# Merged DMA transposes, a wider fp16 ring and a moved copy of x in a cross-attention and routed-FFN kernel

## What is computed

```python
# x: (1, 1024, 128), context q: (1, 6404, 128)
c = layernorm(x)
s = (c @ w_c + b_c)[:, :, None] + (q @ w_q + b_q)[:, None, :] + einsum('bcd,bqd,d->bcq', c, q, w_cq) + b_cq
a = softmax(s, axis=2)
c2q_att = a @ q
b_att = softmax(max(s, axis=2), axis=1)
q2c_att = einsum('bc,bcd->bd', b_att, c)
x = x + concat([c, c2q_att, c * c2q_att, c * q2c_att]) @ W_l.T + b_l
n = layernorm(x)
expert_id = argmax(n @ wr + br)             # 8 experts
x = x + (gelu(n @ w1[e] + b1[e]) @ w2[e] + b2[e]) for e = expert_id of each row
```

## Time and profile before

| | before |
|---|---|
| median of 3 runs | 235.63 us (235.04 to 236.16) |
| the profiled execution's own time | 233.51 us |
| its span | 231.8 us |
| TensorE busy | 198.0 us (85%) |
| VectorE busy | 180.0 us (78%) |
| ScalarE busy | 158.0 us (68%) |
| GpSimd busy | 130.5 us (56%) |
| hardware DMA queue of SyncE | 49.56 MB, 93.2% of the 16 engines' span |

### The profile page before, as it was taken

One profiled execution on the slowest core, in us unless ns is written; L12 is line 12 of the kernel. 1 busy time (PEld: TensorE's weight loads), 2 busy tenths in 40 slices (PEclk: granted clock), 3 DMA queues, 4 the chain that ended last, 5 costly groups with the idle time before them and its releaser, 6 DMA issues.

```text
span 231.8 us, 5012 instructions
## 1 busy us (share of the span) xinstructions
PE 198.0 (85%) x1837; PEld 148.7 (64%) x1837; DVE 180.0 (78%) x393; ACT 158.0 (68%) x249; POOL 130.5 (56%) x179
## 2 busy tenths in 40 slices
PE   0298798995999969999999999899993799799970
PEld 0133356663676736776866767789983799789960
DVE  2789997995997994997997998958847447567770
ACT  2750799994799689399699699689432355667630
POOL 4699405999607987505906988654400740037783
PEclk9999999999999988999999999999995579999997
DMA  6999999899999999999989999969992459999200
GB/s 206 382 277 247 192 298 244 182 221 201 262 193 254 226 203 226 267 170 243 245 193 261 209 204 225 212 141 210 237 285 78 146 200 296 370 365 382 71 21 0
DMA packets 141918, 51.25 MB, mean 221 GB/s; under 512 B 121156, under 2 KB 139733, under 8 KB 141894
## 3 DMA queue, kind: packets, MB, share of 16 engines
q1 hardware_dynamic: 140960, 49.56, 93.2%
q0 software_dynamic: 784, 1.38, 1.7%
q10 hardware_dynamic: 150, 0.00, 0.0%
HBM read 10.22 MB, written 3.75 MB: 60 GB/s over the span
## 4 chain that ended last, share of the span: by engine, by line
PE 42%; DVE 22%; DMA 12%; issue 11%; ACT 9%; POOL 3%; DVEq 0%; ACTq 0%; POOLq 0%
DMA PT<-Phl 10%; DVE S L792 5%; PE psX L1075 5%; PE psS L1055 5%; PE psS L1057 5%; PE psS L1056 5%; ACT S L646 5%; DVE Phl L809 4%; PE psO L1075 4%; ACT Phl L661 3%; PE psS L1288 3%; PE psX L1077 3%; POOL out_x L603 2%; PE psS L1274 2%; PE psO L1077 2%
## 5 line engine op out<-in xcount | busy, mean ns | idle before, releaser
L646 ACT ACTIVATE S<-S,negb 128x1024 f32<-128x1024 f32 x48 | 55.0, 1145 | 14.6 <-DVE negb L800 14.6
L792 DVE TENSOR_SCALAR_CACHE_REDUCE S<-psS 128x1024 f32<-128x1024 f32 x48 | 58.2, 1216 | 8.2 <-PE psS L1057 7.7
L809 DVE TENSOR_TENSOR Phl<-S,Phl 128x1024 f16<-128x1024 f32 x38 | 50.9, 1340 | 7.7 <-ACT Phl L661 7.6
L661 ACT CAST Phl<-S 128x1024 f16<-128x1024 f32 x48 | 50.2, 1045 | 6.1 <-DMA PT<-Phl 4.7
L533 POOL TENSOR_TENSOR Phl<-S,Phl 128x256 f16<-128x256 f32 x40 | 26.2, 685 | 48.6 <-ACT Phl L661 48.6
L1055 PE MATMUL psS<-qT,gh 128*128 128x512 f16 x96 | 37.8, 394 | 3.3 <-DVE gl L769 2.7
L1075 PE MATMUL psO<-qn,PT 128*128 128x256 f16 x204 | 37.4, 277 | 2.5 <-DMA PT<-Phl 2.4
L1075 PE MATMUL psX<-qn,PT 128*128 128x256 f16 x204 | 36.4, 273 | 2.6 <-DMA PT<-Phl 2.6
L1056 PE MATMUL psS<-qT,gh 128*128 128x512 f16 x96 | 37.7, 392 | 0.0
L1057 PE MATMUL psS<-qT,gl 128*128 128x512 f16 x96 | 37.7, 392 | 0.0
L1077 PE MATMUL psO<-qn,PT 128*128 128x128 f16 x204 | 36.0, 222 | 0.0
(11 more groups left out here) (239 smaller groups left out, 424.9 us busy)
## 6 DMA issues: line engine op xcount, KB each, us to landing
PT<-wp SPq DMA_DIRECT2D x8, 512.0 KB, 4.9
stageT<-in_ctxT SPq DMA_DIRECT2D x6, 512.0 KB, 7.3
qn<-wp SPq DMA_DIRECT2D x6, 512.0 KB, 6.8
wp<-in_w SPq DMA_DIRECT2D x4, 512.0 KB, 4.8
stageT<-in_w SPq DMA_DIRECT2D x4, 512.0 KB, 4.7
rows_by_expert<-stageT SPq DMA_DIRECT2D x4, 385.5 KB, 5.3
PT<-Phl SPq DMA_TRANSPOSE x48, 4.1
S<-rows_by_expert SPq DMA_DIRECT2D x2, 258.0 KB, 5.6
```

The lines of the kernel that those rows point to most:

```text
L646: nc.scalar.activation(slot(t, e), slot(t, e), ACT.Exp, bias=negb[:, t:t + 1], accum_out=Lp[:, t * NG + e:t * NG + e + 1]).then_inc(exp_do ...
L661: nc.scalar.copy(hi, slot(t, e)).then_inc(high_done, 1)
L792: nc.vector.tensor_scalar(out=into, in0=bank(u, n)[:, 0:into.shape[1]], scalar1=1.0 / GS, scalar2=None, op0=ALU.mult, op1=ALU.max, accum_o ...
L809: nc.vector.tensor_tensor(lo, slot(t, e), hi, ALU.subtract).then_inc(low_done, 1)
```

## The change

1. `Phl` holds six pieces and the tail side by side, a place for each piece of a row tile. The 8 KB per partition for it come from the scratch of dynamic DMAs (8192 instead of the default). high(t, e) now waits for the landing of the transpose that took the same piece of row tile t-1.
2. A transpose takes a unit: pieces 0 and 1, pieces 2 and 3, pieces 4 to 6 (in the last row tile 4, and 5 with 6). The issue waits for the low halves of all of the unit's pieces, and each W waits for its whole unit. 25 transposes of P take the place of 56, and 4 of the context that of 7.
3. ScalarE copies x into `x_re`; GpSimd adds b_l in place later, behind low(1, 3). evict(1, 1) waits for the copy, not for the sum.
4. Two loads of w1 are issued before the transposes of the context; the load of w2 that belongs to row tile t (1 to 4) is issued behind the last unit of row tile t.

```diff
-        Phl = sb("Phl", [P, PARTS, 2, GR], F16)
-        Ptail = sb("Ptail", [P, 2, TAILP], F16)
+        PW = 2 * GR
+        Phl = sb("Phl", [P, (NG - 1) * PW + 2 * TAILP], F16)
+        Ptail = Phl[:, (NG - 1) * PW:].rearrange("p (a w) -> p a w", a=2)
...
+        QN_UNITS = ((0, 2), (2, 4), (4, 6), (6, 7))
...
+        def pT_units(t):
+
+            return ((0, 2), (2, 4), (4, 5), (5, NG)) if t == T - 1 else ((0, 2), (2, 4), (4, NG))
...
-            def transpose(t, e):
-
-                wait_low(sp, t, e)
+            def transpose(t, g):
+
+                e0, e1 = pT_units(t)[g]
+                for e in range(e0, e1):
+                    wait_low(sp, t, e)
                 if t > 0:
-                    sp.wait_ge(pv_done, (t - 1) * NG + e + 1)
-                src, _, _, dst = piece(t, e)
-                sp.dma_start_transpose(dst, src).then_inc(pT_landed[e], 16)
+                    sp.wait_ge(pv_done, (t - 1) * NG + e1)
+                end = (NG - 1) * PW + 2 * TAILP if e1 == NG else e1 * PW
+                n = len([j for e in range(e0, e1) for j in tiles(e)])
+                sp.dma_start_transpose(PT[:, 2 * e0 * TW:2 * (e0 * TW + n), :],
+                                       Phl[:, e0 * PW:end]).then_inc(pT_landed[g], 16)
...
-            for k in range(H - 1):
-                load_w1(k)
+            load_w1(0)
+            load_w1(1)
+            for g, (n0, n1) in enumerate(QN_UNITS):
...
-            for e in range(NG):
-                transpose(0, e)
-            load_w1(H - 1)
-
-            W2_BEHIND = {(1, 5): 0, (2, 3): 1, (3, 1): 2, (4, 1): 3}
-            for t in range(1, T):
-                for e in range(NG):
-                    transpose(t, e)
-                    if (t, e) in W2_BEHIND:
-                        load_w2(W2_BEHIND[t, e])
+            for t in range(T):
+                for g in range(len(pT_units(t))):
+                    transpose(t, g)
+                if t == 0:
+                    load_w1(H - 1)
+                elif t <= H:
+                    load_w2(t - 1)
...
+            pool.wait_ge(qTl_ready, len(DVE_LOW))
             pool.wait_ge(qTl_pool_ready, len(POOL_LOW))
-            pool.wait_ge(qTl_ready, DVE_LOW.index(4) + 1)
-            pool.wait_ge(x_landed, 16)
-            pool.wait_ge(late_landed, 16 * NLATE)
-            nc.gpsimd.tensor_tensor(x_re, x_sb, blr[:, :].unsqueeze(1).broadcast_to([P, T, D]),
-                                    ALU.add).then_inc(x_re_ready, 1)
-            pool.wait_ge(qTl_ready, len(DVE_LOW))
...
             low_piece(1, 3)
+            pool.wait_ge(x_kept, 1)
+            pool.wait_ge(late_landed, 16 * NLATE)
+            nc.gpsimd.tensor_tensor(x_re, x_re, blr[:, :].unsqueeze(1).broadcast_to([P, T, D]),
+                                    ALU.add).then_inc(x_re_ready, 1)
             split(0)
...
             deviation(2, H, T)
+            act.wait_ge(qTl_ready, DVE_LOW.index(4) + 1)
+            act.wait_ge(qTl_pool_ready, POOL_LOW.index(5) + 1)
+            nc.scalar.copy(x_re, x_sb).then_inc(x_kept, 1)
             act.wait_ge(shift_ready, 1)
...
-                past = t * (NG - 1) + e - PARTS
-                if e == NG - 1 and t > 0:
-                    act.wait_ge(pT_landed[e], 16 * t)
+                if t > 0:
+                    act.wait_ge(pT_landed[pT_unit(t - 1, e)], 16 * t)
                 elif e == NG - 1:
                     act.wait_ge(consts_ready, 5)
-                elif past >= 0:
-                    act.wait_ge(pT_landed[past % (NG - 1)], 16 * (past // (NG - 1) + 1))
...
             def weighted(t, e):
 
-                pe.wait_ge(pT_landed[e], 16 * (t + 1))
+                pe.wait_ge(pT_landed[pT_unit(t, e)], 16 * (t + 1 if t < T - 1 or e < 5 else 1))
...
-    nc = _bacc.Bacc("TRN2", target_bir_lowering=False, num_devices=1)
+    nc = _bacc.Bacc("TRN2", target_bir_lowering=False, num_devices=1, dynamic_dma_scratch_size=8192)
```

More of the change, by code:

```diff
@@ L67, in build @@
     SLOTS = 8
-    PARTS = 4
     BANKS = 3
@@ L183, in build @@
         x2T = S[:, 0, :]
-        hf = parts_ring[:, RING * 2 * F:RING * 4 * F].bitcast(F32).rearrange("p (r f) -> p r f", f=F)
+        hf = Phl[:, RING * 2 * F:RING * 4 * F].bitcast(F32).rearrange("p (r f) -> p r f", f=F)
         xTp = S[:, 1:3, :].rearrange("p r w -> p (r w)")[:, 0:(NB + 1) * P].bitcast(F16)\
@@ L201, in build @@
         x_landed = sem("x_landed")
+        x_kept = sem("x_kept")
         x_re_ready = sem("x_re_ready")
@@ L204, in build @@
         qT_landed = [sem(f"qT_landed{n}") for n in range(NG)]
-        qn_landed = [sem(f"qn_landed{n}") for n in range(NG)]
+        qn_landed = [sem(f"qn_landed{g}") for g in range(4)]
         late_landed = sem("late_landed")
@@ L228, in build @@
         exp_done = sem("exp_done")
-        pT_landed = [sem(f"pT_landed{e}") for e in range(NG)]
+        pT_landed = [sem(f"pT_landed{g}") for g in range(4)]
         high_done = sem("high_done")
@@ L320, in columns, with qn_unit, pT_unit @@
             return buf[:, 0, 0:w], buf[:, 1, 0:w]
+        QN_UNITS = ((0, 2), (2, 4), (4, 6), (6, 7))
+        def qn_unit(n):
+            return min(n // 2, 3)
         def rows_of(n):
-            k = len(tiles(n))
-            buf = qT[:, n, :, :] if n < NG - 1 else qTend[:, :, :]
-            return buf.rearrange("p a w -> p (a w)"), qn[:, 2 * n * TW:2 * n * TW + 2 * k, :]
+            return qn[:, 2 * n * TW:2 * n * TW + 2 * len(tiles(n)), :]
+        def pT_units(t):
+            return ((0, 2), (2, 4), (4, 5), (5, NG)) if t == T - 1 else ((0, 2), (2, 4), (4, NG))
+        def pT_unit(t, e):
+            return [e0 <= e < e1 for e0, e1 in pT_units(t)].index(True)
         def pool_low(t, e):
@@ L349, in bank, with piece @@
             return psS[(u * NG + n) % BANKS]
[L351 to L356, removed]
+        def piece(e):
+            w = cols(e, GR)[1] - e * GR
+            buf = Phl[:, e * PW:(e + 1) * PW].rearrange("p (a w) -> p a w", a=2) if e < NG - 1 else Ptail
+            return buf[:, 0, 0:w], buf[:, 1, 0:w]
         def block_w(b):
@@ L402, in load_w2 @@
                              w2[k * n:(k + 1) * n].rearrange("e (k p) d -> p e k d", p=P)).then_inc(w_landed[H + k], 16)
-            for k in range(H - 1):
-                load_w1(k)
+            load_w1(0)
+            load_w1(1)
+            for g, (n0, n1) in enumerate(QN_UNITS):
+                for n in range(n0, n1):
+                    sp.wait_ge(qTh_ready, n + 1)
+                    if n in DVE_LOW:
+                        sp.wait_ge(qTl_ready, DVE_LOW.index(n) + 1)
+                    else:
+                        sp.wait_ge(qTl_pool_ready, POOL_LOW.index(n) + 1)
+                src = qT[:, n0:n1, :, :].rearrange("p n a w -> p (n a w)") if n1 < NG else \
+                    qTend[:, :, :].rearrange("p a w -> p (a w)")
+                k = sum(len(tiles(n)) for n in range(n0, n1))
+                sp.dma_start_transpose(qn[:, 2 * n0 * TW:2 * (n0 * TW + k), :], src).then_inc(qn_landed[g], 16)
+            load_w1(2)
             for r in (0, 32):
@@ L529, in low_piece @@
                 pool.wait_ge(high_done, t * NG + e + 1)
-                _, hi, lo, _ = piece(t, e)
+                hi, lo = piece(e)
                 for a in range(0, GR, CHUNK):
@@ L651, in high @@
                 act.wait_ge(exp_done, t * NG + e + 1)
-                past = t * (NG - 1) + e - PARTS
-                if e == NG - 1 and t > 0:
-                    act.wait_ge(pT_landed[e], 16 * t)
+                if t > 0:
+                    act.wait_ge(pT_landed[pT_unit(t - 1, e)], 16 * t)
                 elif e == NG - 1:
                     act.wait_ge(consts_ready, 5)
-                elif past >= 0:
-                    act.wait_ge(pT_landed[past % (NG - 1)], 16 * (past // (NG - 1) + 1))
-                _, hi, _, _ = piece(t, e)
+                hi, _ = piece(e)
                 nc.scalar.copy(hi, slot(t, e)).then_inc(high_done, 1)
@@ L783, in scores @@
                     dve.wait_ge(c_late_ready, T - H)
-                    dve.wait_ge(x_re_ready, 1)
+                    dve.wait_ge(x_kept, 1)
                 if n == NG - 1 and u >= 2:
@@ L1061, in weighted @@
             def weighted(t, e):
-                pe.wait_ge(pT_landed[e], 16 * (t + 1))
+                pe.wait_ge(pT_landed[pT_unit(t, e)], 16 * (t + 1 if t < T - 1 or e < 5 else 1))
                 if t == 0:
-                    pe.wait_ge(qn_landed[e], 16)
+                    pe.wait_ge(qn_landed[qn_unit(e)], 16)
                 if t == 0 and e == 0:
@@ L1072, in weighted @@
                 n, acc = len(tiles(e)), psA[t % 2]
-                both = rows_of(e)[1].rearrange("p (a j) d -> p a j d", a=2)
+                both = rows_of(e).rearrange("p (a j) d -> p a j d", a=2)
                 for i, j in enumerate(tiles(e)):
```

11 lines of the change are left out of this document (1 added, 10 removed).

## The result

The changed kernel takes 249.39 us (median of 4 runs, 247.27 to 249.69), the kernel before 235.66 in the same session: a ratio of 1.0565, 95% interval 1.050 to 1.063. It is slower, as forecast, but by 13.7 us instead of 4.0, and above the range. The profiled execution took 249.69 us with a span of 248.0. The ratios leave out the executions of a kernel that are over 1.5% longer than its fastest; the profiled executions of experiments 1 and 8 are of these.

What follows compares the result with a forecast made beforehand. TensorE was taken to set the pace in mid-attention. Terms -1.55 + 0.15 + 1.0 - 1.6 + 3.8 + 2.2 = +4.0 on 233.5 gave 237.5, median 239.6 us; range 237 to 242, eight times in ten 230.5 to 244.5.

Steps and rivals of the forecast that it cites:

- What bounds the kernel: Attention: TensorE sets the pace, turns take about 16.6 us; turns 2 and 4 lose 2.5 us each to late transposes.
- the price of 3.7 us for a load: Turns 2 and 4: a 512 KB weight load ahead of a transpose costs that transpose 3.7 us.
- Price of a merged transpose: Transposes of P: fixed 2.0 us plus about 0.1 a block, so 32 blocks land in 5.5 us, 38 in 6.0.
- Rival A: Faster: 38 blocks land within 4.8 us, so W(t,4) never waits; 230.6 us, chance 0.24.
- Rival B: No change: 38 blocks land in 5.1 us, between 4.8 and 5.4, shrinking the wait at W(t,4); 235.4 us, chance 0.14.
- the term for turns 3 to 7: W(t,4) waits 1.25 us for its unit each turn: turn 3 +1.0, turn 4 -1.6, turns 5 to 7 +3.8.
- part 2: Turns 1 and 2: 0; T(2) at 60.6 against 62.0, so the start's 1.4 us is kept.
- part 4: Last row tile: W(6,4) waits for the last unit of row tile 6, 6.95 us after T(7); +2.2 us.
- the gain of the copy of x: Start: without GpSimd's sum there the shift comes 1.55 us earlier, T(0) goes from 28.2 to 26.7.
- Rival C: Slower still: waits let the clock fall, about 1.7 us each, or w2 loads delay first units; 244 us, chance 0.14.
- The ring and the scratch at 0: Turn 2's old loss only changes its cause; smaller scratch at 21 indirect DMAs costs 0, at most some 2 us.
- the early w1 loads: Start: queued ahead of the context's transposes, which W(0,0) needs only 15 us later; cost 0, other bound 3.7 us.

Runs made afterwards that it cites:

- experiment 1: Changed kernel with one transpose for each piece again, of P and of the context: ratio 0.985 to the kernel before.
- experiment 8: Experiment 1 with the first two w1 loads behind the context's transposes: ratio 0.989 to the kernel before.
- experiment 12: Experiment 1 with only pieces 5 and 6 merged in one transpose of 22 blocks: ratio 0.986 to the kernel before, 232.53 us.
- experiment 11: Kernel before with the ring of six and ScalarE's copy of x, single transposes and all loads as before: ratio 0.996.
- experiment 4: Kernel before with only the ring of six places and the tail, and the smaller scratch: ratio 1.000.
- experiment 2: Changed kernel with units (0,1) (2,3) (4,5) (6) in every row tile: ratio 1.028 to the kernel before, 243.15 us.
- experiment 3: Kernel before with only ScalarE's copy of x and GpSimd's sum moved behind low(1, 3): ratio 0.994.
- experiment 6: Changed kernel with the first two w1 loads back behind the context's transposes: ratio 1.059 to the kernel before.
- experiment 10: Experiment 1 with pieces 0 and 1, and pieces 2 and 3, merged: ratio 1.019 to the kernel before, 240.18 us.
- experiment 7: Changed kernel with 64 one-column matmuls on idle TensorE at the start, to move the instruction packets: ratio 1.047 to the kernel before.

## Why the prediction was right in sign and wrong in size

**What bounds the kernel** held: turns of 16.6 us where nothing waits (experiments 1 and 12), and turn 4 lost its time to a transpose with a weight load ahead of it (experiments 1 and 11). In turn 2 the ring passed such a late landing on to ScalarE (experiment 4), though TensorE waited for it as well, 2.37 us at 56.34. But the price of 3.7 us for a load is a wrong reading of the earlier trace rows: both of these transposes also met a packet of the instruction queue, at 53.29 and 82.77. In the DMA view of before from 53.0 to 55.5 us, inside the transpose issued at 49.00, the same stop stands as in the changed kernel:

```profile
DMA  9999999990100100100901001000001049999999
GB/s 414 266 274 274 524 250 262 258 61 8 12 8 8 12 8 8 12 8 12 16 8 12 8 8 12 8 8 8 12 8 12 8 106 279 299 279 307 283 287 287
...
q8 instruction: 1, 0.02, 2.4%
```

Two transposes of before with a load ahead and no packet, issued at 90.74 and 107.51, landed in 5.4 and 6.0 us. The second:

```profile
PT<-Phl SPq DMA_TRANSPOSE x1, 6.0
```

So a load ahead costs about 2 us, and the rest of the 3.7 is the packet.

**Price of a merged transpose:** 5.5 and 6.0 forecast for 32 and 38 blocks, 5.6 to 5.8 and 6.2 to 6.4 measured where nothing disturbs them. The upper figure for contiguous transposes in the Trainium skill (DMA: Bandwidth & Descriptors, Latency and other measured facts), weighed in the prediction, is not borne out: the stream stays at 280 to 290 GB/s in the long ones. Rivals A and B, which needed a landing under 4.8 or 5.4, fall with this.

**The step that failed** is the term for turns 3 to 7 (and with it parts 2 and 4): it took the landing of a lone transpose for that of all. The trace of before already held the other kind. Over the transposes of P in the profile of before, the 16 with an instruction packet in flight landed in 5.3 us by median, the 40 without in 3.9; in the changed kernel 7 take 7.7 and 18 take 5.9. Of the 16 in before ten still landed 1.0 to 3.3 us ahead of the first matmul of their W. The last unit of the change has nothing to spare: TensorE waits for it even when it is on time (1.08 and 1.13 us), and a packet in it adds 1.4 us (7.7 against 6.3) or 2.5 us (8.8). The lost 12 us of span beyond the forecast 4, from the table and the rows above:

- T(0), +1.0: the gain of the copy of x is there, the twin of L747 takes 0.16 us (timeline below), but T(0) is later than forecast. Experiments 1, 2 and 3 have it at 26.4, 26.7 and 26.8, and over all profiles of kernels with this copy it lies between 26.3 and 27.7, so this is the spread of the start as far as is known. The c_sb on VectorE, 2.24 us at 7.12 instead of 1.47, is not the reason: in experiment 3 it took 2.6.
- Turn 2, +2.3: W(0,0) came at 41.55, forecast 38.8, after 4.96 us of idling. Of these 2.7 us 1.0 is T(0), 1.3 is SyncE, which came to unit (0,0) only after the context's transposes and the third w1 load, and 0.4 the landing. The clock fell to half with it (the first row of the windows below).
- Turns 3 and 4, +2.9: together they took 38.0 us, 4.8 more than two turns of 16.6, and TensorE idled 4.6 us in them: 1.83 ahead of W(1,4), which the prediction had on time, 1.20 ahead of W(2,0) and 1.58 ahead of W(2,4). The unit of W(2,0) stood behind the w2 load and took 9.2 us, with a packet in it at 75.54; the prediction named this bound, up to 1.5 us, and took 0. That of W(2,4) had the packet at 88.86.
- Turn 5, +3.6: the packet in the unit of W(3,4), a wait of 3.73 us, and the clock (second row).
- T(7) to the last W, +1.7: W(6,4) came 6.9 us after T(7), exactly as forecast, but W(7,2) waited 1.30 us for a unit that took 8.2 us with a packet in it. Another 0.7 us went behind the last W, and the reason for it is open.

VectorE's and ScalarE's timeline of the changed kernel at the start (the third and fourth row are the new copy and the c_sb activations behind it):

```profile
7.12 2.24 DVE L771 TENSOR_SCALAR c_sb<-S,mv,rstd 128x128 f32<-128x128 f32 x4
...
22.36 0.16 DVE L761 TENSOR_TENSOR sc<-rstd 128x4 f32<-128x4 f32 x1
...
21.13 1.04 ACT L651 COPY stageT<-S 128x1024 f32<-128x1024 f32 x1 [4.61 <-DVE qT L790]
...
23.35 1.65 ACT L654 ACTIVATE c_sb<-S,sc,rstd 128x128 f32<-128x128 f32 x4 [1.18 <-DVE sc L848]
```

The copy is hidden: 1.18 us of idling are still left behind it. Windows of the changed kernel, columns as in the earlier trace rows:

```profile
38.90:45.80 6.90, 4.25 (x27) 3.45 (x28) 5.78 (x10) 6.50 (x12) 6.40 (x10) 0.51 1.00 227
110.60:114.00 3.40, 2.67 (x17) 2.19 (x18) 0.00 (x0) 3.37 (x5) 2.92 (x6) 0.50 1.05 253
```

The granted clock is at half (1.2 GHz) there; each time it fell in the course of a TensorE wait, those of 4.96 and 3.73 us that ended at 41.55 and 111.33. With the waits of 1.1 to 1.8 us in the other turns it stayed at full (2.4 GHz). Rival C had this mechanism and named two or three falls; it was the nearest case, with two falls in the attention, but its 244 us have no packets in them, and it had a chance of 0.14. Its reading of before is off: the wait that ended at 85.05 and was followed by a fall was 2.23 us long, and the one of 2.4 (2.37 us, at 56.34) was followed by none.

**VectorE's share.** The wait list of the changed kernel shows the same chain from its other end: VectorE now waits for scores, where before had 7.7 us in 7 waits.

```profile
DVE S L806 <- PE psS L1071: 24.4, 19, 5.1
...
PEld psO L1089 <- DMA PT<-Phl: 14.3, 6, 5.0
...
PEld psX L1089 <- DMA PT<-Phl: 10.3, 6, 4.2
```

**The ring and the scratch at 0** held in the whole time (experiment 4). So did the early w1 loads (experiments 6 and 8), but not for the reason given: W(0,0) does not miss the context's transposes, it misses its own, which stand behind them in SyncE's stream (1.3 us late in the change, 4.7 us in experiment 1). The first units' 0.5 us in a turn held (experiment 10); that merging them makes turn 2 3 to 4 us longer did not.

Left open: why turn 3 of experiment 4 takes 17.2 us, why T(0) spreads by more than 1 us, and how much of the packet's cost depends on the place in the transpose at which it falls. A kernel without instruction packets was not tried.

## What to carry to other kernels

Before transfers are merged, take for each the time from the last input to the first use, not the mean load of the queue: a merged transfer is issued with its latest input and needed by its earliest reader, and where that reader sits in the stream of the bounding engine every microsecond is paid each turn. If anything, merge where the first reader is late anyway (pieces 5 and 6), and cost a landing by the worst ones in the trace, not by the lone ones. Look, too, at what else was in flight before a late landing is put down to what stood ahead of it. Moving four w2 loads took 2.7 to 3.3 us out of turn 4; 31 transfers fewer gained nothing.

## What the runs showed of the hardware

- A 16 KB packet of the instruction queue stops a running DMA transpose on all sixteen engines: for 1.9 us in the stretch shown, and 1.4 us by the medians of before (5.3 against 3.9 us). When experiment 7 moved the packets, the last units of row tiles 2 and 3 landed in 6.3 and 7.2 us instead of 7.7 and 8.8. A packet comes once for some 260 TensorE instructions. The Trainium skill (Runtime: NRT & Kernel Launch, Instruction fetch mechanics) says that an engine's sequencer fetches blocks of 16 KiB, 256 instructions, through a DMA queue of its own, and calls this mostly hidden; the trace agrees with the block size, and shows that the transposes pay for it.
- GpSimd's sum of 128x1024 held up a VectorE operation of four elements for 1.5 us; without it the same operation took 0.16 us.
- A 512 KB load issued right ahead of a transpose of 16 blocks delays it by about 2 us: 5.4 and 6.0 us to landing in before, 5.9 to 6.2 in experiment 1, where no packet fell into it. With a packet as well it is 3.4 to 3.6 us over the 3.9 (7.3 and 7.5 us in before), and 9.2 us for 32 blocks after.
- Turn 1, in which no W holds up a bank, took 14.7 us with the granted clock at full in before, and 15.9 us in experiment 4 with it at half from 28.3 to 34.0 us.
